# Queries and keys of a causal attention layer projected transposed: rotation, norms and bf16 parts on tile pairs instead of on token rows

## What is computed

```python
h = h + _L0_ffn_ref(...)            # its last step: o @ dequant(w_down).T
qkv = layernorm(h) @ qkv_w.T        # q, k, v: 16 heads of 16
q = _apply_rot(q, cos, sin)         # (x1*cos + x2*sin, -x1*sin + x2*cos), halves of 8 dims
k = _apply_rot(k, cos, sin)
outs.append(_sdpa(q[:, :6], k[:, :6], v[:, :6], 1.0 / math.sqrt(HD)))       # heads 0-5
tq = jnp.sqrt(1.0 / curv + jnp.sum(q * q, axis=-1, keepdims=True))          # heads 6-9
tk = jnp.sqrt(1.0 / curv + jnp.sum(k * k, axis=-1, keepdims=True))
qn = q / jnp.maximum(jnp.linalg.norm(q, axis=-1, keepdims=True), 1e-12)     # heads 10-15
kn = k / jnp.maximum(jnp.linalg.norm(k, axis=-1, keepdims=True), 1e-12)
```

## Time and profile before

| | us |
|---|---|
| median of 3 executions | 5732.23 (5721.1 to 5742.0) |
| the profiled execution | 5748.39 |
| its span, from first to last instruction | 5746.7 |
| `phase_f1`: first rotation of batch 0 to that of batch 31 | 1544.39 to 2226.18 |
| in 1560 to 2240 (680 us): TensorE busy | 591.61 |
| same: VectorE busy | 542.57 |
| same: ScalarE busy | 251.88 |
| same: mean granted TensorE clock | 0.90 of full |

### The profile page before, as it was taken

The page is one execution under the profiler, slowest core; times in us unless marked ns, Lnnn a source line. Parts: engine busy times, 40 slices in busy tenths (PEclk is TensorE's granted clock), DMA queues, the critical chain, the costliest instruction groups (busy, mean ns, idle before and its releaser), DMA issues. The chain is left out here.

```text
span 5746.7 us, 99792 instructions
## 1 busy us (share of the span) xinstructions
PE 4422.5 (77%) x26575; PEld 2884.0 (50%) x26575; DVE 3816.5 (66%) x9299; ACT 2478.7 (43%) x5698; POOL 596.5 (10%) x928
## 2 busy tenths in 40 slices
PE   6999788300388885878787776776999998689898
PEld 5777566200255553555555555554555554344444
DVE  4555333588687877777767764555777777477776
ACT  2222333565333333677777762222666666200000
POOL 0111000000000001000000001111111111122221
PEclk9999899655699997777777787887999999899998
DMA  2222233679644443222222225555333333211110
GB/s 81 74 75 68 105 140 139 196 240 396 229 132 124 132 124 91 62 71 71 71 71 71 71 52 144 156 156 139 85 91 92 92 90 88 63 46 47 49 47 25
DMA packets 380380, 617.00 MB, mean 107 GB/s; under 512 B 43575, under 2 KB 310389, under 8 KB 380277
## 3 DMA queue, kind: packets, MB, share of 16 engines
q1 hardware_dynamic: 367956, 614.35, 36.6%
q0 software_dynamic: 12320, 1.40, 0.2%
HBM read 345.02 MB, written 269.21 MB: 107 GB/s over the span
## 5 line engine op out<-in xcount | busy, mean ns | idle before, releaser
L1670 DVE TENSOR_REDUCE e_neg<-ps 91x1 f32<-91x273 f32 x1536 | 571.8, 427 | 139.2 <-PE ps L1491 131.8
L1603 ACT ACTIVATE e_probT<-ps 91x273 f32<-91x273 f32 x1536 | 491.6, 392 | 291.7 <-PE ps L1491 290.9
L1218 PE MATMUL ps<-k_downT,f_o 128*91 128x256 f32 x1152 | 259.7, 385 | 455.9 <-DVE f_o L1126 455.7
L2345 PE MATMUL ps<-m_we,m_xT 128*128 128x512 f32 x1104 | 530.8, 630 | 0.0
L1218 PEld LDWEIGHTS ps<-k_downT,f_o 128*91 128x91 f32 x1152 | 182.8, 161 | 524.5 <-issue 456.9
L1489 PE MATMUL ps<-c_mask_kq,c_identb 91*91 91x91 bf16 x1536 | 322.7, 241 | 105.9 <-ACT g_probT L1603 74.3
L1491 PE MATMUL ps<-e_k,e_q 96*91 96x273 bf16 x1536 | 344.3, 306 | 62.9 <-DMA e_k<-s_parts 28.1
L2279 DVE SCALAR_TENSOR_TENSOR m_acc<-ps,m_weight,m_acc 128x256 f32<-128x256 f32 x552 | 261.7, 481 | 185.7 <-PE ps L2345 175.9
L1491 PE MATMUL ps<-g_q,g_k 102*91 102x273 bf16 (+5 forms) x1536 | 328.5, 294 | 50.6 <-DVEq L1676 49.9
L2345 PEld LDWEIGHTS ps<-m_we,m_xT 128*128 128x128 f32 x1104 | 214.8, 202 | 227.9 <-issue 213.5
L1491 PE MATMUL ps<-e_q,e_k 128*91 128x273 bf16 x1536 | 285.7, 290 | 40.1 <-DMA e_q<-e_shift 38.2
(11 more groups left out here) (306 smaller groups left out, 9733.9 us busy)
## 6 DMA issues: line engine op xcount, KB each, us to landing
s_gate<-b_gu SPq DMA_DIRECT2D x32, 819.0 KB, 4.7
s_up<-b_gu SPq DMA_DIRECT2D x32, 819.0 KB, 6.1
c_g<-s_gate SPq DMA_DIRECT2D x32, 819.0 KB, 7.2
s_gated<-c_g SPq DMA_DIRECT2D x32, 819.0 KB, 8.6
d_g<-s_gated SPq DMA_DIRECT2D x32, 819.0 KB, 10.4
d_u<-s_up SPq DMA_DIRECT2D x32, 819.0 KB, 10.7
s_o<-d_o SPq DMA_DIRECT2D x32, 819.0 KB
f_o<-s_o SPq DMA_DIRECT2D x32, 819.0 KB, 4.8
```

Of the source, the lines that this page charges most:

```text
L1218: last = nc.tensor.matmul(ps[0:R, t // 2, (t % 2) * D:(t % 2 + 1) * D], o[:, u, k, t * R:(t + 1) * R], downT[:, k, :], start=(k == 0), sto ...
L1603: nc.scalar.activation(probT[0:R, p % 8, b, :], src, ACT.Exp, scale=float(HD) ** 0.5 if kinds[h] == COS else 1.0)\
L1670: last = nc.vector.tensor_reduce(neg[:, u, t, h:h + 1], src, AX.X, ALU.max, negate=True)
L2345: last = nc.tensor.matmul(ps[0:R, EBANK[m % 4], :], xT[:, u, k, t * R:(t + 1) * R], we[:, k, 2 * p:2 * p + 2, :].rearrange("p e d -> p (e ...
```

## The change

Queries and keys now come out of `project` already transposed: the weights are the stationary operand, so that 128 channels (8 dims of 16 heads) lie on the partitions and the 273 tokens on the columns. Four such tiles (queries and keys, lower and upper half of the dims) fill banks 4 to 7. The two halves of a head that a rotation mixes are then two tiles on the same partitions. `rotate` is two products over all four tiles (128x1092) with tables `f_rot`, and one sum and one difference (128x546 each). The squares of all heads are summed over the dims by four matmuls with a 128x128 matrix `f_select` of zeros and ones (`sums`, into banks 4 and 5), which also spreads each head's sum over all of its dims. `guard` moves from GpSimd to VectorE. The root and the reciprocal are now taken of 128x546 values, and `unit` becomes 1 in the heads that are not scaled. `turn_heads` is gone. The parts are taken from `f_qk` in SBUF, two tiles in an instruction; tq and tk have parts of their own (`f_xparts`, 16 rows). `quantise_o` and `residual` run one batch further ahead, `down` is cut in two steps, and SP's order is turned round.

```diff
-        TURN = (2, 3, 1)
+        Y, TURNED, HEADS, SUMS = 0, 2, 4, 4
...
             def rotate(n, u, i):
-                dve.wait_ge(S["turn"].sem, S["turn"].before(n))
-                for t in range(NT):
...
-                    nc.vector.tensor_tensor(rc[:, u], x, cos, ALU.mult)
...
-                for t in range(NT):
...
-                    nc.vector.reduce_sum(ss[:, u, 2 * t:2 * t + 2, :], sq[:, u].rearrange("p a d h -> p a h d"), AX.X).then_inc(S["ss"].sem, 1)
+                dve.wait_ge(S["qk"].sem, S["qk"].at(n))
...
+                for to, table in ((rc, 0), (rs, 1)):
+                    nc.vector.tensor_tensor(to[:], x, rot[:, table].unsqueeze(1).unsqueeze(1)
+                                            .to_broadcast([128, 2, HALVES, T]), ALU.mult).then_inc(S["rc"].sem, 1)
+                dve.wait_ge(S["rc"].sem, S["rc"].at(n))
+                nc.vector.tensor_tensor(qk[:, u, :, 0], rc[:, :, 0], rs[:, :, 1], ALU.add).then_inc(S["rot"].sem, 1)
+                nc.vector.tensor_tensor(qk[:, u, :, 1], rc[:, :, 1], rs[:, :, 0], ALU.subtract)\
+                    .then_inc(S["rot"].sem, 1)
+
+            def guard(n, u, i):
+                dve.wait_ge(S["ss"].sem, S["ss"].at(n))
+                dve.wait_ge(S["rest"].sem, S["rest"].before(n))
+                nc.vector.tensor_scalar(norm[:, u], ps[:, SUMS:SUMS + 2, 0:T], floor[:], 1e-24, ALU.add, ALU.max)\
+                    .then_inc(S["cap"].sem, 1)
 
             def scale_heads(n, u, i):
                 dve.wait_ge(S["norm"].sem, S["norm"].at(n))
...
-                nc.vector.reciprocal(norm[:, u, :, 4:NSCALED], norm[:, u, :, 4:NSCALED]).then_inc(S["inv"].sem, 1)
...
+                nc.vector.reciprocal(unit[:], norm[:, u]).then_inc(S["inv"].sem, 1)
...
+                nc.vector.tensor_scalar(unit[:], unit[:], select[:, 128:129], select[:, 129:130], ALU.mult, ALU.add)\
+                    .then_inc(S["unit"].sem, 1)
...
+                nc.vector.tensor_tensor(qk[:, u], qk[:, u], unit[:].unsqueeze(2).to_broadcast([128, 2, HALVES, T]),
+                                        ALU.mult).then_inc(S["scaled"].sem, 1)
...
-            pipeline(dve, NB, ((scale_heads, -1), (quantise_o, 2), (residual, 1), (lower_parts, -1), (normalise, 1),
-                               (rotate, 0)))
+            pipeline(dve, NB, ((guard, -1), (scale_heads, -1), (statistics, 1), (first_rest, -1), (normalise, 1),
+                               (lower_parts, -1), (rotate, 0), (quantise_o, 3), (residual, 2)))
...
+            def squares(n, u, i):
+                act.wait_ge(S["rot"].sem, S["rot"].at(n))
+                act.wait_ge(S["ss"].sem, S["ss"].at(previous(n)))
+                nc.scalar.activation(sq[:], qk[:, u], ACT.Square).then_inc(S["sq"].sem, 1)
...
+                for a in range(2):
+                    nc.scalar.copy(parts[:, u, a, :, part_place(a, 0), :], qk[:, u, a]).then_inc(S["hi"].sem, 1)
...
+                nc.scalar.copy(parts[:, u, :, :, 1, :], rest[:]).then_inc(S["mid"].sem, 1)
+                nc.scalar.copy(xparts[:, u, :, 1], xrest[:]).then_inc(S["mid"].sem, 1)
...
+            pipeline(act, NB, ((roots, -1), (copy_x, 0), (upper_parts, -1), (middle_parts, -1), (round_o, 3),
+                               (copy_values, 0), (squares, 0)))
...
+            def sums(n, u, i):
+                pe.wait_ge(S["sq"].sem, S["sq"].at(n))
+                for a in range(2):
+                    for half in range(HALVES):
+                        last = nc.tensor.matmul(ps[:, SUMS + a, 0:T], select[:, 0:128], sq[:, a, half, :],
+                                                start=(half == 0), stop=(half == HALVES - 1))
+                last.then_inc(S["ss"].sem, 1)
...
-            pipeline(pe, NB, ((turn_x, 0), (down, 1), (turn_heads, -1), (project, 0)))
+            pipeline(pe, NB, ((turn_x, 0), (down_first, 2), (project, 0), (values, 0), (down_others, 2), (sums, 0)))
...
-            pipeline(sp, NB, ((next_o, 1), (store_h, 1), (store_parts, -1), (next_h, 1), (store_v, 0)))
+            pipeline(sp, NB, ((store_v, 0), (next_h, 1), (store_parts, -1), (store_h, 2), (next_o, 2)))
```

More of the change, by code:

```diff
@@ L1104, in second_part @@
-            def second_part(n, u, j):
-                rows = ROWS[j]
-                act.wait_ge(S["rest"].sem, S["rest"].at(n, j + 1))
-                nc.scalar.copy(parts[0:rows, u, j, 1, :], rest[0:rows, u, j % 2]).then_inc(S["mid"].sem, 1)
-            pipeline(act, NB, ((copy_x, 0), (round_o, 2), (upper_parts, -1), (values_and_squares, 0), (norms, 0)))
+                act.wait_ge(S["norm"].sem, S["norm"].at(n))
+                nc.scalar.copy(xparts[:, u, 0, 0], norm[0:H, u, 0]).then_inc(S["hi"].sem, 1)
@@ new lines, in first_rest @@
+            def first_rest(n, u, i):
+                dve.wait_ge(S["lo"].sem, S["lo"].at(previous(n)))
+                dve.wait_ge(S["hi"].sem, S["hi"].at(n))
+                nc.vector.tensor_tensor(xrest[:, 0], norm[0:H, u, 0], xparts[:, u, 0, 0], ALU.subtract)\
+                    .then_inc(S["rest"].sem, 1)
+                nc.vector.scalar_tensor_tensor(out=xrest[:, 1], in0=norm[0:H, u, 1], scalar=-1.0,
+                                               in1=xparts[:, u, 1, 0], op0=ALU.mult, op1=ALU.subtract)\
+                    .then_inc(S["rest"].sem, 1)
+                for a in range(2):
+                    nc.vector.tensor_tensor(rest[:, a], qk[:, u, a], parts[:, u, a, :, part_place(a, 0), :],
+                                            ALU.subtract).then_inc(S["rest"].sem, 1)
@@ new lines, in down, with down_first @@
+            def down(u, t):
+                for k in range(FT):
+                    last = nc.tensor.matmul(ps[0:R, Y + t // 2, (t % 2) * D:(t % 2 + 1) * D],
+                                            o[:, u, k, t * R:(t + 1) * R], downT[:, k, :],
+                                            start=(k == 0), stop=(k == FT - 1))
+                return last
+            def down_first(n, u, i):
+                pe.wait_ge(S["oq"].sem, S["oq"].at(n))
+                pe.wait_ge(S["h2"].sem, S["h2"].at(previous(n)))
+                down(u, 0)
@@ L1228, in project @@
             def project(n, u, i):
                 pe.wait_ge(S["xT_out"].sem, S["xT_out"].at(n))
[L1230 removed]
+                pe.wait_ge(S["cap"].sem, S["cap"].at(previous(n)))
+                for j in range(4):
+                    for k in range(CT):
+                        last = nc.tensor.matmul(ps[:, HEADS + j, 0:T], wqkv[:, k, j * 128:(j + 1) * 128],
+                                                xT[:, u, k, :], start=(k == 0), stop=(k == CT - 1))
```

274 lines of the change are left out of this document (102 added, 172 removed).

## The result

The changed kernel takes 5813.6 us (median of 4, 5809.04 to 5815.03) against 5735.08 for the kernel before, timed beside it: ratio 1.0139, 95% interval 1.0118 to 1.0159. The change made the kernel slower, as forecast, by more than forecast, and the time lies 8 us above the range. The profiled execution took 5809.04 us.

What follows compares the result with a forecast made beforehand. The stage was taken as a loop through TensorE and VectorE, bound by its length: 23.3 us a turn against 22.0. 31 turns +40, tail +7, lead-in -2 made +45, so 5777 us on the median; range 5705 to 5806.

Steps and rivals of the forecast that it cites:

- the sums at 4.0 us at the low level: Four `sums` matmuls closing the turn: taken at 4.3 us at TensorE's low clock, 2.0 to 2.2 at full clock.
- the tail: After the last rotation starts, up to SP's last store: 29.9 us against 22.6 before, so +7.3.
- `round_o` without a wait for `f_o`: SP's new order: `f_o` lands 5 to 6 us into the next turn, `round_o` wants it at 12, so hidden.
- rival 1: TensorE runs the sums at full clock: turn 21.2 us, program 5710 us; chance 0.18.
- Rival 2: VectorE's reciprocal is dearer at 546 columns: 4.7 us, +1.1 a turn, +35 in all, 5812 us; chance 0.12.
- rival 3: TensorE's clock alternates, turns of 21.2 and 23.3 us mixed; at half and half 22.25, program 5745 us; chance 0.16.
- `normalise` (1.04) lies under it: VectorE's 1.04 us `normalise` is covered by ScalarE's 1.75 us of middle parts, leaving a new wait of 0.8.
- on GpSimd only work goes away: Said of GpSimd in the new turn: it only loses work; no cost was given for it.
- the hand-overs: Passing work between engines in the turn: 0.03 to 0.05 us each, read from gaps in the trace.
- the lead-in: Before the first rotation: 1.7 us shorter, from a shorter, earlier first projection against more `down` and 0.35 MB more to load.
- TensorE's idleness: TensorE's wait ahead of the sums each turn: 3.8 us, or 2.8 if the low clock costs it 1 us more.
- the median of three is 16 us under it, and I put the sum on the median: Base of the total: the profiled execution took 5748.4 us; +45 makes 5793 for that, 5777 on the median.

## Why the prediction was right in kind and too small

| from the start of `guard` | predicted | measured |
|---|---|---|
| reciprocal starts | 1.45 | 1.68 |
| scaling ends | 6.9 | 7.18 |
| rests end | 10.3 | 10.62 |
| low parts start | 12.05 | 12.60 |
| rotation starts | 13.95 | 14.51 |
| squares end | 19.0 | 19.54 |
| next `guard` | 23.3 | 23.73 |

**Right.** The order of the chain, the reciprocal (3.57 us for a predicted 3.6: 6.25 ns for each column beyond the 48 of the earlier trace rows), the sums at 4.0 us at the low level, the tail (+7.4 for +7.3), a stage clock under 0.90, and `round_o` without a wait for `f_o`. The busy time of a turn came out a little lower than forecast, 18.05 us on VectorE for 19 and 8.1 on ScalarE for 9. I had put 18 in 100 on the sums at full clock (rival 1, turn 21.2): with the clock kept up the turn is 21.85, and in this order it doesn't stay up by itself. Rival 2 named 5812 us, within 2 of the measured time, and is false all the same: the reciprocal took 3.57 us, not 4.7. That its number came so close is chance; other things brought the time there. The alternating clock (rival 3) appears only without the reciprocal.

**The step that failed first: "`normalise` (1.04) lies under it", and "on GpSimd only work goes away".** I counted what GpSimd runs and not what its remaining instruction would meet. In the kernel before, its sum of 91x3 ran beside a pair of rests that read one operand from PSUM, and took 0.19 us:

```profile
1893.07 0.76 DVE L1190 TENSOR_TENSOR f_rest<-ps,f_parts 128x273 f32<-128x273 f32 x2
...
1893.24 0.19 POOL L118 TENSOR_TENSOR f_var_eps<-f_mv,c_eps 91x3 f32<-91x3 f32 x1 [6.56 <-DVE f_mv L102]
```

The rests now read both operands from SBUF, and L110 runs beside them. It takes 1.97 us, and `normalise` is 1.0 late. The middle parts cover most of that: the low parts start 0.30 us after ScalarE's last middle part, and 0.04 where nothing holds them up, as in the order with the statistics late. So this step cost about 0.27 us a turn, some 8 us in all (an estimate from these two gaps over 29 turns). That order gained 0.4 a turn because its rests also ended 0.12 sooner.

**Mis-sized: the hand-overs.** The reciprocal starts 0.23 late: `guard` took 0.79 instead of 0.72, and each crossing to ScalarE and back about 0.1 instead of 0.03 to 0.05. The 0.23 alone are some 7 us over 31 turns. Together with GpSimd's share, and the sums a little shorter than forecast, the turn of 23.3 becomes 23.65 in the mean: 51.4 us for 40.

**Wrong in sign: the lead-in, "I make it 1.7 shorter".** It is 1.9 longer. I counted the projection and the bytes, but not the eight curvature loads at the end of SP's first loads, nor that VectorE waits 8.77 us for them ahead of its first quantisation, which starts 14.7 us into the stage instead of 10.6. Issued elsewhere they give back 4.6.

**Too cautious: TensorE's idleness, "3.8 us, or 2.8".** It is 5.1. TensorE's own part of the turn took 14.7 us (predicted 15.2), it began 0.2 us ahead of `guard`, and the squares came 0.5 later. This changed no number, since the level was low either way.

**The sum and its base, "the median of three is 16 us under it, and I put the sum on the median".** The terms are 51.4 + 7.4 + 1.9 = 60.8 (with rounding) against +45: 16 us short. The base was low as well: I took 5732, the median of three executions, and the kernel before had medians of 5745.91, 5748.91 and 5743.24 in the later comparisons. 5746 and 60.8 make 5807, which is what the repeat of the changed kernel measured (5806.67). So of the 37 us between 5777 and 5813.6 about 16 are the terms, 14 the base, and the last 7 separate two medians of the same changed kernel; they stay open. On the base that I took, the measured terms would have made 5793.

**Where the gain went.** The work of a turn stayed about level on TensorE and VectorE (above), so there was no gain in the busy sums to begin with. The layout replaced reductions and transposes, which lay beside other work, by a serial chain, and the order put squares and sums at its very end with `guard` first behind them. The same instructions with the chain ahead of the independent work are 1.1% faster than the kernel before: the loss comes from the order that was chosen with the layout. What the kernel before would gain from an order of its own was not tried, so this doesn't show which layout is the better one.

## What to carry to other kernels

In a loop written out by hand, price its length from one link back to itself, not the busy sums; then place the chain that crosses engines ahead of the work that can wait, which here was worth 122 us, TensorE's clock included, where nothing was computed differently. An instruction that is priced by the column, such as the reciprocal, grows with the layout even when the numbers it needs don't (36 columns became 546). When steps are reordered, look also at what runs on the neighbour engine beside them.

## What the hardware showed unexpectedly

- GpSimd's sum of 91x3 took 1.97 us in each of 29 turns where it started beside a run of VectorE instructions with two operands in SBUF, and ended with that run (1894.58 against 1894.52 in the turn above); with VectorE idle, or beside an instruction that reads one operand from PSUM, it took 0.19. The Trainium skill (SBUF — State Buffer, "Who interferes with whom") states that a VectorE instruction with two SBUF inputs contends with a GpSimd instruction that reads SBUF, and that the order of issue decides which of them blocks. The trace agrees: GpSimd's started 0.14 us behind the first of the run, and four VectorE instructions in a row let it in between none of them.
- The level of TensorE's clock for the same sums: full (2.11 us) behind 1.24 and 1.67 us of idleness, low (3.79 and 4.01) behind 2.19 and 5.11. But in the run without the reciprocal one set of sums took 2.11 us behind 2.61 us of idleness, so the length of the idle time just ahead does not decide alone.
- The clock fell while TensorE stood idle, not when it started again: 1.00 in 1898.4 to 1900.4, 0.50 from 1901.0 on, sums from 1903.49. After the low sums it was back at the full level within the next transposes (0.64 and 0.73 us for six), some 4 us after the restart, where the prediction had read 6.4 from the earlier trace rows of the kernel before.
